# The 8-head attention pass of a four-layer graph network: two small products gated earlier, two groups of query products issued later

## The reference

```python
qe = q[:, c, :]; ke = k[:, r, :]; ve = v[:, r, :]       # c = destination, r = source of an edge
sim = jnp.einsum('hed,hed->eh', qe, ke) * scale
m = jax.ops.segment_max(sim, c, num_segments=bs)
p = jnp.exp(sim - m[c])
s = jax.ops.segment_sum(p, c, num_segments=bs)
attn = p / s[c]                                          # then times ve, summed per destination, times Wo
```

## Time and profile before

| what | value |
|---|---|
| median of three runs | 6995.06 us |
| the profiled execution, its own time | 6978.94 us |
| its span | 6977.1 us |
| busy PE, DVE, POOL, ACT | 4606.5, 4396.6, 4515.6, 2546.8 us (66, 63, 65, 37% of the span) |
| the 8-head pass: 55 forward scans, first and last start | 1519.5 and 2995.8 us |
| longest line of the chain that ended last | PE L977, 21% |

### The profile page before, as it was taken

How to read it: one execution, slowest core, us unless ns; L and a number is a source line. 1 busy time by engine, 2 the same in 40 slices (tenths; PEclk the granted TensorE clock), 3 DMA queues, 4 the chain that set the end, 5 groups by cost and what they waited for, 6 DMA issues and landing times.

```text
span 6977.1 us, 103168 instructions
## 1 busy us (share of the span) xinstructions
PE 4606.5 (66%) x17172; PEld 3026.2 (43%) x17173; DVE 4396.6 (63%) x11645; ACT 2546.8 (37%) x6805; POOL 4515.6 (65%) x4928
## 2 busy tenths in 40 slices
PE   3555555877777777784777777566776735555556
PEld 2444444544444444463444444444444423343333
DVE  5555554558888888874666666655565564444546
ACT  0000000545555655654555555554554540000004
POOL 5777776036666666617777775377777747777770
PEclk8777777988888878896777777777777767777776
DMA  3333335257777777745444444344444543333333
GB/s 86 105 105 105 105 104 102 90 189 221 222 219 222 219 222 223 214 123 149 137 131 132 132 131 92 99 133 135 131 131 136 119 137 105 105 105 105 105 103 89
DMA packets 499186, 962.75 MB, mean 138 GB/s; under 512 B 105403, under 2 KB 296510, under 8 KB 491616
## 3 DMA queue, kind: packets, MB, share of 16 engines
q0 software_dynamic: 240064, 696.46, 36.9%
q1 hardware_dynamic: 258749, 262.93, 11.6%
HBM read 895.74 MB, written 64.63 MB: 138 GB/s over the span
## 4 chain that ended last, share of the span: by engine, by line
PE 36%; POOL 20%; issue 18%; DVE 15%; DVEq 4%; DMA 4%; ACT 3%; ACTq 1%; POOLq 0%; SPq 0%
PE bank L977 21%; POOL ring L707 19%; DVE acc L1439 4%; PE bank L1027 3%; DMA ring<-g_t,stage 2%; PE bank L1221 2%; DVE ring L1651 2%; DVE acc L1436 2%; PE bank L1174 1%; DVE aux L1500 1%; PE bank L1042 1%; DVE ohc L1445 1%; PE bank L1043 1%; PE bank L1044 1%; PE bank L1200 1%
## 5 line engine op out<-in xcount | busy, mean ns | idle before, releaser
L977 PE MATMUL bank<-ring,ohc 128*128 128x256 f32 (+3 forms) x8800 | 3212.4, 517 | 1550.7 <-DMA ring<-xs_t,stage 432.4
L977 PEld LDWEIGHTS bank<-ring,ohc 128*128 128x128 f32 x8800 | 2063.5, 252 | 2500.1 <-issue 1066.7
L1439 DVE TENSOR_TENSOR acc<-acc,bank 128x256 f32 (+2 forms) x3520 | 1485.2, 422 | 1498.3 <-PE bank L977 1368.0
L707 POOL DMA_INDIRECT ring<-g_t,stage x1760 | 1715.7, 975 | 521.7 <-issue 466.2
L707 POOL DMA_INDIRECT ring<-kv_t,stage x880 | 918.2, 1043 | 555.3 <-PE bank L977 325.8
L707 POOL DMA_INDIRECT ring<-in_x,stage x880 | 835.2, 949 | 263.8 <-issue 256.7
L707 POOL DMA_INDIRECT ring<-xs_t,stage x880 | 834.1, 948 | 260.9 <-issue 258.3
L840 ACT ACTIVATE aux<-bank 128x512 f32<-128x512 f32 (+1 forms) x26 | 14.9, 572 | 2225.5 <-PE bank L1163 2225.5
L766 ACT ACTIVATE ohc<-iota,rel_c 128x128 f32<-128x128 f32 x1760 | 557.2, 388 | 67.7 <-PE bank L977 66.6
L812 ACT ACTIVATE cl<-cl 128x1 f32<-128x1 f32 (+3 forms) x111 | 22.5, 203 | 1502.6 <-DVE mx L1644 909.7
L1436 DVE SCALAR_TENSOR_TENSOR acc<-acc,aux,bank 128x264 f32 x880 | 422.9, 481 | 119.9 <-PE bank L977 106.8
(11 more groups left out here) (299 smaller groups left out, 4954.1 us busy)
## 6 DMA issues: line engine op xcount, KB each, us to landing
aux<-relb_t SPq DMA_DIRECT2D x56, 1024.0 KB
aux<-q_t SPq DMA_DIRECT2D x880, 64.0 KB
relx<-relb_t SPq DMA_DIRECT2D x55, 512.0 KB
ring<-g_t,stage POOLq DMA_INDIRECT x1760, 2.8
x<-ring SPq DMA_DIRECT2D x21, 896.0 KB, 4.2
ring<-x SPq DMA_DIRECT2D x21, 896.0 KB, 9.5
mk<-mk SPq DMA_DIRECT2D x445, 32.1 KB
ring<-in_x,stage POOLq DMA_INDIRECT x880, 2.8
```

The source lines that it names most:

```text
L707: g_.indirect_dma_start(out=rings[L][:, slot, 0:W], out_offset=None, in_=table[L][:, :], in_offset=bass.IndirectOffsetOnAxis(ap=stage[:, s ...
L977: return mm(agp[k % AB][:, 0:width], ohc[:, hot, :], rg[:, slot, vo:vo + width], start=True, stop=True)
L1439: tt(win, win, agp[k % AGP[L]][:, 0:width], ALU.add).then_inc(p["added"], 1)
```

## The change

On PE alone, and in L = 1 alone. `rows_of` is replaced by two functions. `tails_of` makes the tails' two products from the forward scan (`fw`) instead of the backward one, behind the semaphore `fwd` instead of `ch1`; `heads_of` makes the heads' product behind `ch1` and releases `row`. (The backward scan starts from the last column of the forward one, so both hold the same number there.) The query products r = 0 of the next batch, which stood between sums 11 and 12, now stand behind sum 15. Those of r = 1, which stood behind sum 15, now stand behind `turn_back`.

```diff
--- before.py
+++ after.py
@@ -1080,6 +1080,18 @@
                             mm(m0[0:R, 0:128], ident[0:R, 0:R], mk[0:R, par, 385:513], start=False, stop=True)\
                                 .then_inc(p["st"], 1)
 
+                        def tails_of():
+
+                            gate(pe, p["fwd"], b + 1)
+                            mm(m1[0:1, tail:tail + HW], fw[0:R, 127:128], sel[0:R, 0:HW], start=True, stop=False)
+                            mm(m1[0:1, tail:tail + HW], ones[0:1, 0:1], fprow[0:1, fp_at, 0:HW], start=False, stop=True)
+
+                        def heads_of():
+
+                            gate(pe, p["ch1"], b + 1)
+                            mm(m1[0:1, head:head + R], mx[0:R, 0:1], ident[0:R, 0:R], start=True, stop=True)\
+                                .then_inc(p["row"], 1)
+
                         def rows_of():
 
                             gate(pe, p["ch1"], b + (past(L) + 1))
@@ -1115,18 +1127,18 @@
                                 turn_scores()
                             sums_of(9, 10)
                             if scores:
-                                rows_of()
-                            sums_of(10, 12)
-                            if feed:
-                                dest_rows(nb, npar, 0)
-                            sums_of(12, 14)
+                                tails_of()
+                                heads_of()
+                            sums_of(10, 14)
                             if scores:
                                 cols_of()
                             sums_of(14, 16)
                             if feed:
+                                dest_rows(nb, npar, 0)
+                            if scores:
+                                turn_back()
+                            if feed:
                                 dest_rows(nb, npar, 1)
-                            if scores:
-                                turn_back()
                         else:
                             sums_of(0, 16)
                             if scores:
```

More of the change, by code:

```diff
@@ L1126, in batch @@
                             if feed:
-                                dest_rows(nb, npar, 1)
+                                dest_rows(nb, npar, 0)
                             if scores:
                                 turn_back()
+                            if feed:
+                                dest_rows(nb, npar, 1)
                         else:
```

## The result

The changed kernel takes 7021.47 us (median of six runs, 7012.42 to 7030.66) against 6994.88 us before (median of six). The ratio is 1.0041 with a 95% interval of 1.0031 to 1.0051: 27 us slower. The forecast was 6993 us and no change; the measured time lies inside its range, in the case that had a chance of 0.27 (slower), not in the one that was forecast.

The account below looks back on a forecast made before the run. DVE's work and pauses were followed as the bound, with the clock holding the loop in step. The parts summed to 26.65 us per batch, 6960 us; in step cancelled this, leaving 2 us off the ends: 6993 us, range 6950 to 7040.

Parts of the forecast that it names:

- the sum with the clock left alone: 8-head pass: 27.3 - 1.55 + 0.9 = 26.65 us per batch if the clock's rise stays where it is.
- The loop is held by the clock: 8-head pass: the chip sets the clock's rise; a quicker loop runs ahead of it and slows until in step.
- with a mean near the old 27.3: 8-head pass: batches of unequal length, some near 26.6 and some near 28.5 us, averaging near the old 27.3.
- in step, no change: Forecast case: the pass keeps its 27.3 us mean, only its ends move; 6993 us, chance 0.42.
- the 0.9 us that the late loads give back: Before add 0: query loads of r = 2 leave later, so 0.9 of the 1.55 us gain is lost per batch.
- the slower rival: r = 0 at half clock before `pair(0)`, 2.5 us in every second batch: 7027 us, chance 0.27.
- PE then stands idle before it, where the clock may fall a second time: Slower rival's second half: PE idles before r = 2 from about 21 to 22.7, where the clock may fall again.
- by a few us: Ends of the 8-head pass, in the case in step: they alone move, with 2 us taken off.
- one case in which PE stood waiting: Query loads: the only wait seen in the trace, 4.71 us from first load to first product.
- The faster case: Clock does not bind: 6960 us, or 6913 with loads in time; needs an early rise in nearly all batches; chance 0.26.
- the rise comes later than 6.45 us behind the scan: Sign of being right: in the pass the clock rises later behind the forward scan than the old 6.45 us.

Follow-up runs that it names:

- e10: Kernel before with only the tails' gate: tails ahead of heads, gated on the forward scan, nothing moved; 6991.27 us, ratio 1.0004.
- e6: The change with 16 slots for query loads instead of 8; 7001.81 us against 7002.55, ratio 0.9995.
- e8: Kernel before with three products of no use behind each of sums 4 to 7; 6878.81 us, ratio 0.9849.
- e9: Kernel before with only the query products r = 0 moved behind sum 15; 7011.2 us against 6987.99, ratio 1.0035.
- e5: The change with three products of no use behind each of sums 4 to 7; 6929.85 us, ratio 0.9888.
- e1: The change with 16 slots for query loads, on the chips with the longer times (before takes 8493.95 us); ratio 1.0099.

## Why the prediction was wrong

- **The prices of the parts were mostly right.** `pair(0)` comes 9.39 us behind the scan in the mean of the 32 batches with r = 0 at full clock, against 9.4 worked out; from first load to first product pass 4.63 us against 4.71; the pause before add 0 is 0.98 us in the mean of the 49 batches against 0.9; the pause before add 12 is gone. These 32 batches take 26.67 us, where the sum with the clock left alone said 26.65. One part was too large: `rows_forward` comes 2.78 us behind the scan instead of 3.05, 0.27 earlier and not 0.45, and waits 0.55 in the mean where under 0.5 was expected.
- **The loop is held by the clock: right, and larger than said.** Before, the clock rises 6.43 to 6.56 us behind the scan in each of the 49 batches. e10 and e6 keep the mean at 27.29 and 27.33 us with quite different orders, and e8 frees the old order from 27.31 to 25.05. By the rule cited from the Trainium skill ("TensorE: Matmul & The Clock Gate", on what happens in the gate) a schedule of the chip's own sets when the clock is judged; a mean that stays the same through such edits agrees with it.
- **The step that failed** is "with a mean near the old 27.3", in the case "in step, no change". In it the 0.9 us that the late loads give back was put at nothing: the step would swallow it like any other time. Without late loads that holds (27.33, e6); with them the mean is 27.67, 0.34 us more in each of 49 batches. A batch that has r = 0 at half clock takes 29.54 us (17 of 49), without late loads 28.24 (28 of 49, e6); the others take 26.67 and 26.12. The loop did answer, long batches became fewer, but not by enough. What happened is the slower rival, to its place and its second half ("PE then stands idle before it, where the clock may fall a second time"): in 15 of 49 batches the clock falls between that pause and add 0, 13 of them long ones, and in the 12 in which query products behind the pause are slow too the pause before add 0 is 1.69 us.
- **That 7021 lies so near the rival's 7027 is in part luck.** It was priced at 2.5 us in every second batch, 32 us, all of it in the batches. Measured are 17 long batches of 49, 2.87 us longer than the short ones, which puts the 49 batches 17.7 us above before; most of the rest comes from the end of the pass.
- **How much is the pause and how much the fall is not settled.** The four long batches without a second fall average 28.91 us, the 13 with it 29.74, those of e6 without late loads 28.24; by these few, an estimate, 0.7 us of a long batch is the pause and 0.8 the fall. e9 warns against a simple sum: there PE waits longer for loads (50.4 us in 400) and the clock falls in twice as many batches, yet with two long ones alone the mean is 27.42. Why the change has more long batches than e9 stays open.
- **The other part of the same step** is the end of the pass. The case in step let the ends move "by a few us" and took 2 us off; the last two batches wait for loads up to 7 us, and the change pays 8.6 us there, a third of the loss. The three kernels with r = 0 moved and eight slots (the change, e5, e9) take 66.7 to 67.5 us for these two batches, the seven others 56.0 to 61.8. The trace of before already had such waits there, up to 4.32 us, so the prediction's "one case in which PE stood waiting" for loads misread it. What makes loads so late at the end was not looked into.
- **The faster case** failed by its own condition: it needed an early rise in nearly all batches, and in 17 of 49 the clock is still down when r = 0 starts. The forecast that the rise comes later than 6.45 us behind the scan holds for these 17 (10.7 to 11.7), and not for all of the 32 short ones, where it lies between 5.0 and 7.2. In the short one shown the column products, 6.1 us behind the scan, are at full clock (0.38 us, where the long batch has 0.58), so that `limit_before` starts at 6.72; in the long one the rise comes at about 2112.4, 10.7 behind.

## What to carry to other kernels

When a loop's length stays the same while work moves within it, and the granted clock falls and rises at the same place in each round, suspect that the clock sets the length: here a pause removed in one place came back in another (e10). Try a few products of no use in the idle stretch where the clock falls before judging any order (here -1.5% for the old order, and -2.1% with the change and the slots, on chips where before takes about 6990 us; on the others the same products brought nothing or a loss). When a step that frees buffers is moved later, follow the loads that wait for those buffers to their first use; here they cost 0.9 us per batch with the clock kept up, twice what the new order gains (0.44), and more slots were the missing half of the change.

## What was not expected of the hardware

- Twelve small products per batch of no use, spread over four pauses, raise the granted clock of the pass from 0.79 to 0.96, and the kernel gets 1.5% faster for 660 products more (ratio to before 0.9888 against 1.0041, each on its own chip).
- The same kernel takes 6986 to 7003 us on some chips and 8382 to 8515 us on others. There the 8-head pass is longer and so is what stands ahead of it and behind it (1770 us to the first forward scan in e1, 1526 in the change). What makes it so, the traces don't show.
